# Turning the feed-forward rows with VectorE and a trip through DRAM instead of TensorE

## The chip, the cores and the metric

The kernel runs on one core of a Trainium2 chip. The metric is device time in microseconds (us), from one launch, as the median of repeated runs. The engines are TensorE (PE; its weight loads are listed as PEld), VectorE (DVE), ScalarE (ACT), GpSimd (POOL) and SyncE (SP), which here issues every DMA. Each engine works through its own instructions in the order in which they were written and waits on semaphores.

## The reference, cut to what matters

Eight sequences of 2048 rows of 256 numbers go through one layer: attention with a decay `0.9 ** |n - m|` on the softmax, then a gated feed-forward with 4-bit quantised operands (`F` = 704).

```python
x = x + attention(layernorm(x))
q4 = fp4_quant_dequant            # blocks of 16 along the last dimension
xn = layernorm(x)
h = silu(q4(xn) @ q4(w_gate).T) * (q4(xn) @ q4(w_up).T)      # rows x 704
x = x + q4(h) @ q4(w_down).T                                  # needs q4(h) with its columns on partitions
```

## The kernel before

A first stage (to about 310 us) makes keys, queries and values of all sequences and prepares the weights. Then come 128 tiles of 128 rows (`B` = 8 sequences of `T` = 16 tiles). A product in fp32 precision is made of three passes over an upper and a lower part of each operand (`PASSES`), so every operand that was transposed into PSUM is copied once by ScalarE (`upper`, line 793) and once subtracted by VectorE (`lower`, line 1226).

The tiles are software-pipelined by hand. Every engine has a function `step(at, s)`, called for s = 0 to 15 of each sequence; s - 1 and so on count into the sequence before. What follows is the order of each engine within a step, which is what the argument needs:

- **TensorE**: `attend_begun(s-1)` (transposes of the first two groups of decayed probabilities of tile s-1), `scores(s)` (24 matmuls), then `attend(s-1)`: for each group g of at most four key blocks, wait until its lower part is there (`copied`), its matmuls, and the transposes of group g+2 behind them; `x_transposed(s-2)` comes behind group 0; `h_transposed(s-5, 0)` and `(s-5, 1)` (4 and 2 transposes of the quantised hidden rows `hq`, line 675) come behind later groups. Then `gate_up(s-2)` (18 matmuls, after `xqT` is copied) and `down(s-5)` (17 matmuls, after `hT` is copied).
- **VectorE**: `maxima(s, 0)`, lower parts of groups 0 and 1 of tile s-1, `maxima(s, 1)` with the negated maximum `nmax`, lower part of `xqT`, lower parts of groups 2 and 3, of `hT` (2 instructions), `h_levels(s-3)`, `residual(s-1)`, then `x_scales` and `x_levels(s-1)` with `h_made(s-2)` between them, then `result(s-5)`.
- **ScalarE**: `queries(s+1)`, upper parts of groups 0 and 1, of `xqT`, of the other groups, of `hT` (2 instructions), `exponentials(s)` (two, each from `nmax`), `gate(s-2)` with table loads around it.
- **GpSimd**: `queries(s+1)`, `decays(s)` (after both exponentials of s), `values` in half of the steps, `x_quantised(s-1)` (after `x_levels(s-1)` of VectorE), `h_quantised(s-3)`, which ends with `hq_ready`, `h_scaled(s-2)`.
- **SyncE**: `load_q(s+2)`, value and edge loads, `store(s-5)` after its result, `load_x(s)`.

A sequence of 16 tiles has 8 to 14 key blocks a tile (tile t attends blocks t-7 to t+7; tiles 7 and 8 save one). In groups of four, the tiles 1 to 4 and 11 to 14 have three groups, the tiles 5 to 10 four. Tiles 0 and 15 have 8 blocks in groups of 2, 3 and 3. Three PSUM banks (`RING`) go round for all transposes and the gate and up products.

Of the kernel before, what the change touches and what calls it, by code (L numbers as in the profile page):

```python
# [8 lines left out]
F32 = mybir.dt.float32  # L9
# [37 lines left out]
XR, LAG, LATER = 8, 5, 3  # L47
# [39 lines left out]
def groups(t):  # L87

    bs = blocks_of(t)
    size = CT if 0 < t < T - 1 else CT - 1  # L90
    first = len(bs) % size or size
    return [bs[:first]] + [bs[i:i + size] for i in range(first, len(bs), size)]


def plan_slots():
# [6 lines left out]
    def step(s, has, weights=False):  # L102
# [12 lines left out]
        for g in range(max(len(gs), 1)):  # L115
            if g == 0 and has(s - 2):
                take("xqT", s - 2)
            if g + 2 < len(gs):
                take("pT", s - 1, g + 2)
            for h in range(2):  # L120
                if g == min(max(len(gs) - LATER, 0) + h, max(len(gs), 1) - 1) and has(s - LAG):
                    take("hT", s - LAG, h)
# [16 lines left out]
def build(nc, X, WQ, WK, WV, WG, WU, WD, rot_tab, decay_tab, eye, out):  # L139
# [5 lines left out]
    with ExitStack() as ctx:  # L145
# [17 lines left out]
        q_dram = nc.dram_tensor("q_dram", (B, NC, P, KT, CH), F32, kind="Internal").ap()  # L163

# [7 lines left out]
        hq = [hq_buf[:, i * FT:(i + 1) * FT] for i in range(2)]  # L172
# [50 lines left out]
        probs = sb("probs", [P, L])  # L223

# [31 lines left out]
        hq_step, hv_ready, hg_ready, hq_ready = sem("hq_step"), sem("hv_ready"), sem("hg_ready"), sem("hq_ready")  # L256
        NSTEP_W, NSTEP_LN2, NSTEP_XQ, NSTEP_HQ = 5, 2, 6, 5
# [26 lines left out]
        def tile(at, t):  # L284

            return at[0] * T + t

# [60 lines left out]
        def _(sp):  # L348
# [115 lines left out]

            def step(j, s, is_first, more):
# [37 lines left out]
            for t in range(T - LAG, T):  # L503
                store(B - 1, t)
# [4 lines left out]
        def _(pe):  # L509
# [120 lines left out]
            def attend(at, t, meanwhile, later):  # L630
                if not has(at, t):
                    meanwhile()
                    later(0)
                    later(1)
# [5 lines left out]
                for g, bs in enumerate(gs):  # L640
# [23 lines left out]
                    for h in range(2):  # L664
                        if g == min(max(len(gs) - LATER, 0) + h, len(gs) - 1):
                            later(h)

            def h_transposed(at, t, h):
                if has(at, t):
                    for ks in (range(0, CT), range(CT, HK))[h:h + 1]:  # L670
                        if h == 0:
                            pe.wait_ge(hq_ready, tile(at, t) + 1)
                        dst = slot(at, "hT", t, h)
                        for j, k in enumerate(ks):
                            mm = pe.transpose(dst[:, j * P:(j + 1) * P], hq[t % 2][:, k * P:(k + 1) * P], ident[:])  # L675
                        mm.then_inc(filled, 1)
# [9 lines left out]
            def down(at, t):  # L686
                if has(at, t):
                    copied(at, "hT", t, 1)
# [11 lines left out]
            def step(at, s):  # L700
# [8 lines left out]
                attend(at, s - 1, lambda: x_transposed(at, s - 2), lambda h: h_transposed(at, s - LAG, h))  # L709
# [13 lines left out]
        def _(act):  # L723
# [87 lines left out]
            def h_transposed(at, t):  # L811
                if has(at, t):
                    for h, n in enumerate((CT, HK - CT)):
                        upper(hT[0][:, h * CT:h * CT + n, :].rearrange("p k t -> p (k t)"),
                              bank(at, "hT", t, h)[:, 0:n * P], at, "hT", t, h)
# [43 lines left out]
            def step(at, s):  # L859
# [3 lines left out]
                attend(at, s - 1, range(min(n, 2)))  # L863
                begins = s == 0 and at[2] is first_plan
# [8 lines left out]
                h_transposed(at, s - LAG)  # L873
# [19 lines left out]
        def _(pool):  # L893
# [84 lines left out]
            def decays(at, s, meanwhile):  # L978
# [4 lines left out]
                for g, bs in enumerate(groups(s)):  # L983
# [15 lines left out]
                    op.then_inc(decayed, 1)  # L999

# [14 lines left out]
            def h_quantised(at, t):  # L1015
                if has(at, t):
# [3 lines left out]
                    if has(at, t - 2):  # L1020
                        pool.wait_ge(filled, nth(at, "hT", t - 2, 1) + 1)
# [3 lines left out]
                    pool.tensor_tensor(hq[t % 2][:, F - HALF:FT].rearrange("p (a b k) -> p a b k", a=2, k=QB), last, scale, ALU.mult)  # L1025
# [399 lines left out]
```

## Time and profile before

| | |
|---|---|
| median of 3 runs | 2549.42 us (2548.14 to 2549.66) |
| span of the profiled execution, first to last instruction | 2546.6 us |
| own device time of the profiled execution | not listed; the median is 2.8 us above the span |
| one sequence of 16 tiles in the middle | 275.62 us |
| first stage | about 310 us |
| tail without scores | from 2504 us on |

Groups of rows name line, engine and operation, then output <- input with shapes. Times in a timeline are us from the start of the span. Busy time is the sum of the instructions of an engine; a timeline row that ends in brackets says how long its engine had been idle and what ended that.

### The profile page before, as it was taken

The numbers are of one execution on the slowest core, as the hardware profiler recorded it, in microseconds if no ns is written. First come the engines' busy times: TensorE is split into PE (matmuls) and PEld (weight loads), VectorE is DVE, ScalarE is ACT, GpSimd is POOL, SyncE is SP. The second block draws the span as 40 slices with busy tenths as digits, with TensorE's granted clock in tenths as the row PEclk, the third lists the DMA queues.
The fourth block names the chain that finished last, engine by engine and source line by source line (L and its number), as shares of the span: only waits on it lengthen the run. The fifth ranks groups of instructions, "written<-read, shape, count | busy, mean of one in ns | idle before, by whom it ended". The sixth has DMA issues, their size and how long they took to land.

```text
span 2546.6 us, 51904 instructions
## 1 busy us (share of the span) xinstructions
PE 2518.4 (99%) x16160; PEld 2290.0 (90%) x16160; DVE 2140.9 (84%) x4759; ACT 1489.8 (59%) x2966; POOL 1816.8 (71%) x1929
## 2 busy tenths in 40 slices
PE   8999999999999999999999999999999999999997
PEld 7888879999999999999999999999999999999996
DVE  8999878888878888888888888888888888888886
ACT  5766565656555655566565656565556655555654
POOL 6999956667767676667766776677666776677665
PEclk9999999999999999999999999999999999999999
DMA  8878511122111311131112111131113111211110
GB/s 285 302 271 299 186 50 30 34 86 66 38 40 45 107 37 42 34 106 42 42 34 91 62 38 40 45 107 39 42 34 106 41 42 34 95 58 38 40 38 22
DMA packets 163473, 203.27 MB, mean 80 GB/s; under 512 B 15184, under 2 KB 116752, under 8 KB 163216
## 3 DMA queue, kind: packets, MB, share of 16 engines
q1 hardware_dynamic: 163216, 200.01, 24.1%
q8 instruction: 141, 2.31, 0.4%
q14 instruction: 116, 0.95, 0.1%
HBM read 103.42 MB, written 77.59 MB: 71 GB/s over the span
## 4 chain that ended last, share of the span: by engine, by line
PE 85%; POOL 0%; DVE 0%; issue 0%; ACT 0%; POOLq 0%
PE score L516 27%; PE acc L655 19%; PE ring L516 19%; PE acc L516 9%; PE ring L622 6%; PE ring L675 3%; PE acc L697 1%; PE ring L613 1%; DVE hT L1226 0%; POOL probs L998 0%; ACT probs L823 0%; ACT hT L793 0%; POOL h_buf L1019 0%; POOL xv L1004 0%; POOL h_buf L1013 0%
## 5 line engine op out<-in xcount | busy, mean ns | idle before, releaser
L516 PE MATMUL score<-keys,q_st 128*128 128x512 f32 x3072 | 733.7, 394 | 3.0 <-ACT probs L823 2.6
L516 PEld LDWEIGHTS score<-keys,q_st 128*128 128x128 f32 x3072 | 567.0, 188 | 117.8 <-issue 3.0
L998 POOL TENSOR_TENSOR probs<-probs,decay 128x512 f32<-128x512 f32 (+3 forms) x416 | 450.7, 1097 | 197.5 <-ACT probs L823 197.5
L655 PE MATMUL acc<-vals,pT 128*128 128x256 f32 x3984 | 554.6, 286 | 0.8 <-DVE pT L1226 0.8
L516 PE MATMUL ring<-w_gu,xqT 128*128 128x512 f32 (+1 forms) x2304 | 509.1, 374 | 0.0
L655 PEld LDWEIGHTS acc<-vals,pT 128*128 128x128 f32 x3984 | 498.1, 189 | 7.3 <-DVE pT L1226 2.0
L516 PEld LDWEIGHTS ring<-w_gu,xqT 128*128 128x128 f32 x2304 | 419.0, 188 | 63.6 <-DVE xqT L1226 0.4
L793 ACT ACTIVATE xqT<-ring 128x256 fp32r<-128x256 f32 x128 | 49.3, 385 | 706.9 <-PE ring L613 706.9
L1239 DVE TENSOR_REDUCE smax<-score 128x1 f32<-128x1024 f32 x256 | 312.8, 1222 | 95.6 <-PE score L516 94.1
L1226 DVE TENSOR_TENSOR pT<-ring,pT 128x512 fp32r<-128x512 f32 (+3 forms) x432 | 248.7, 600 | 66.7 <-ACT pT L793 65.5
L1004 POOL TENSOR_TENSOR xv<-xv,xe 128x256 f32<-128x256 f32 x128 | 94.4, 737 | 269.1 <-DVE xv L1079 269.1
L823 ACT ACTIVATE probs<-score,nmax 128x1024 f32<-128x1024 f32 x256 | 282.8, 1116 | 2.1 <-DVE nmax L1242 2.0
L793 ACT ACTIVATE pT<-ring 128x512 fp32r<-128x512 f32 (+3 forms) x432 | 218.7, 527 | 74.8 <-PE ring L622 66.6
L516 PE MATMUL acc<-w_dn,hT 128*128 128x256 f32 x1920 | 240.9, 277 | 4.7 <-DVE hT L1226 4.6
L516 PEld LDWEIGHTS acc<-w_dn,hT 128*128 128x128 f32 x1920 | 236.7, 188 | 5.8 <-DVE hT L1226 5.3
L1019 POOL TENSOR_TENSOR h_buf<-h_buf 128x704 f32<-128x704 f32 x128 | 219.0, 1711 | 4.3 <-DVE h_buf L1079 4.3
L1322 DVE TENSOR_TENSOR h_buf<-h_buf,ring 128x256 f32<-128x256 f32 (+1 forms) x384 | 144.2, 376 | 76.2 <-ACT h_buf L849 76.0
L793 ACT ACTIVATE hT<-ring 128x512 fp32r<-128x512 f32 (+1 forms) x256 | 125.0, 490 | 123.1 <-PE ring L675 123.1
L1226 DVE TENSOR_TENSOR hT<-ring,hT 128x512 fp32r<-128x512 f32 (+1 forms) x256 | 141.3, 553 | 64.9 <-ACT hT L793 64.8
L622 PE MATMUL ring<-ident,probs 128*128 128x128 f32 x1328 | 194.8, 273 | 0.2 <-DVE w_gu L1231 0.2
L516 PE MATMUL score<-xT,w_in 128*128 128x512 f32 x768 | 188.3, 394 | 2.3 <-DVE xT L1107 2.3
L1013 POOL TENSOR_TENSOR h_buf<-h_buf,hrs 128x704 f32<-128x704 f32 x128 | 178.2, 1392 | 0.0
(133 smaller groups left out, 4470.0 us busy)
## 6 DMA issues: line engine op xcount, KB each, us to landing
k_dram<-keys SPq DMA_DIRECT2D x56, 512.0 KB, 4.5
keys<-k_dram SPq DMA_DIRECT2D x56, 512.0 KB, 7.3
edge<-vals SPq DMA_DIRECT2D x288, 64.0 KB, 2.1
q_raw<-q_dram SPq DMA_DIRECT2D x129, 128.0 KB, 2.6
x_in<-X SPq DMA_DIRECT2D x32, 512.0 KB, 4.5
q_dram<-q_stage SPq DMA_DIRECT2D x32, 512.0 KB, 5.4
x_res<-X SPq DMA_DIRECT2D x128, 128.0 KB, 2.1
out<-x_res SPq DMA_DIRECT2D x128, 128.0 KB, 1.7
```

The source lines that it names most:

```text
L516: mm = pe.matmul(dst, stat(a, k), mov(m, k), start=i == 0, stop=ends and i == n - 1)
L622: mm = pe.transpose(dst[:, n * P:(n + 1) * P], source, ident[:])
L655: mm = pe.matmul(pv_out, pT[g % 2][:, a, j * P:(j + 1) * P], edge[places[m]][:] if kb in edges else vals[m][:, kb, :], start=i == 0, stop= ...
L793: act.activation(dst, src, ACT.Copy).then_inc(hi_done, 1)
L823: act.activation(probs[:, h * 2 * CH:(h + 1) * 2 * CH].rearrange("p (j n) -> p j n", j=2), score[:, 2 * h:2 * h + 2, :], ACT.Exp, bias=nma ...
L998: op = pool.tensor_tensor(probs[:, k0:k1], probs[:, k0:k1], decay[:, off + k0:off + k1], ALU.mult)
L1004: pool.tensor_tensor(xv[:], xv[:], xe[:], ALU.subtract).then_inc(x_levelled, 1)
L1013: pool.tensor_tensor(blocks(hv[t % 2]), blocks(hv[t % 2]), spread(hrs[:], HB), ALU.mult).then_inc(hv_ready, 1)
L1019: pool.tensor_tensor(hv[t % 2], hv[t % 2], he[t % 2], ALU.subtract).then_inc(h_levelled, 1)
L1226: dve.tensor_tensor(dst, src, hi.bitcast(F32), ALU.subtract).then_inc(freed, 1)
L1239: dve.tensor_reduce(smax[:, h:h + 1], score[:, 2 * h:2 * h + 2, :], AX.XY, ALU.max).then_inc(maxed, 1)
L1322: dve.tensor_tensor(hv[t % 2][:, p0:p0 + w], silu[t % 2][:, p0:p0 + w], bank(at, "gu", t, p)[:, w:2 * w], ALU.mult).then_inc(freed, 1)
```

## The change

The hidden rows are no longer transposed by TensorE. For each tile: VectorE turns `hq` (128 rows by 768 columns) in blocks of 32 by 32 in one instruction (`h_turned_blocks(s-4)`, between the lower part of group 1 and `maxima(s, 1)`); SyncE writes the result to DRAM, waits for it, and reads it back with four DMAs, one per 32 columns of each chunk, into `hqT` (`rows_turned(s-4)`, behind `load_q(s+2)`); ScalarE makes the upper part of all six chunks in one instruction from SBUF (`h_transposed(s-5)`, now behind groups 0 and 1 and ahead of the exponentials); GpSimd makes the lower part in one instruction (`h_lower(s+1-5)`, behind `decays(s)` and `values` and ahead of `x_quantised(s-1)`). `hq` has one buffer in place of two. Tile 0 has two groups of four.

```diff
-    size = CT if 0 < t < T - 1 else CT - 1
+    size = CT if t < T - 1 else CT - 1
...
+            def rows_turned(j, t):
+                g, i = j * T + t, t % 2
+                sp.wait_ge(h_turned, g + 1)
...
+                sp.dma_start(h_dram[i], h_turn.rearrange("p (c r) -> p c r", c=CT)).then_inc(turn_out, 16)
+                sp.wait_ge(turn_out, (g + 1) * 16)
+                for c in range(CT):
+                    sp.dma_start(hqT[i][c * QUAD:(c + 1) * QUAD, :, :], h_dram[i, :, c, :].rearrange("(a i) r -> i a r", a=CT)).then_inc(hqT_back[i], 16)
...
+                if s >= TURNED or not is_first:
+                    rows_turned(j, s - TURNED)
...
TensorE:
-                            mm = pe.transpose(dst[:, j * P:(j + 1) * P], hq[t % 2][:, k * P:(k + 1) * P], ident[:])
...
-                    copied(at, "hT", t, 1)
+                    pe.wait_ge(h_split, tile(at, t) + 1)
ScalarE, h_transposed(at, t):
-                        upper(hT[0][:, h * CT:h * CT + n, :].rearrange("p k t -> p (k t)"),
-                              bank(at, "hT", t, h)[:, 0:n * P], at, "hT", t, h)
+                    act.wait_ge(hqT_back[t % 2], halves(at, t) * CT * 16)
+                    if has(at, t - 1):
+                        act.wait_ge(dn_done, tile(at, t))
+                    act.activation(chunks(hT[0][:]), quads(hqT[t % 2][:]), ACT.Copy).then_inc(h_upper, 1)
...
                 attend(at, s - 1, range(min(n, 2)))
+                h_transposed(at, s - LAG)
GpSimd:
+            def h_lower(at, t):
+                if has(at, t):
+                    pool.wait_ge(h_upper, tile(at, t) + 1)
+                    pool.tensor_tensor(chunks(hT[1][:]), quads(hqT[t % 2][:]), chunks(hT[0][:]).bitcast(F32), ALU.subtract).then_inc(h_split, 1)
...
+                h_lower(at, s + 1 - LAG)
                 x_quantised(at, s - 1)
                 h_quantised(at, s - 3)
VectorE:
+            def h_turned_blocks(at, t):
+                if has(at, t):
+                    dve.wait_ge(hq_ready, tile(at, t) + 1)
+                    if has(at, t - 1):
+                        dve.wait_ge(turn_out, tile(at, t) * 16)
+                    dve.transpose(h_turn..., hq...).then_inc(h_turned, 1)
...
                 maxima(at, s, 0)
                 attend(at, s - 1, range(min(n, 2)))
+                h_turned_blocks(at, s - TURNED)
                 maxima(at, s, 1)
...
-                for h in range(2):
-                    h_transposed(at, s - LAG, h)
```

## Rows read from the trace of the kernel before

**Rows 1.** The page's busy times and its granted TensorE clock in 40 slices.

```profile
PE 2518.4 (99%) x16160; PEld 2290.0 (90%) x16160; DVE 2140.9 (84%) x4759; ACT 1489.8 (59%) x2966; POOL 1816.8 (71%) x1929
...
PEclk9999999999999999999999999999999999999999
```

**Rows 2.** Windows of one sequence: us, then busy time of each engine.

```profile
1243.50:1519.12 275.62, 275.62 (x1788) 252.24 (x1787) 230.40 (x519) 160.41 (x318) 191.54 (x223) 1.00 0.18 56
```

**Rows 3.** Timeline of the step that attends tile 5: start us, us, engine, line.

```profile
1500.27 0.56 PEld L622 LDWEIGHTS ring<-ident,probs 128*128 128x128 f32 x5
...
1501.26 0.75 ACT L793 ACTIVATE pT<-ring 128x128 fp32r<-128x128 f32 x2
...
1503.90 0.74 POOL L1004 TENSOR_TENSOR xv<-xv,xe 128x256 f32<-128x256 f32 x1 [1.17 <-DVE xv L1079]
...
1505.33 0.63 SPq L382 DMA_DIRECT2D q_raw<-q_dram  x1
...
1506.58 1.22 DVE L1239 TENSOR_REDUCE smax<-score 128x1 f32<-128x1024 f32 x1 [0.51 <-PE score L516]
...
1507.58 1.28 POOL L1026 TENSOR_TENSOR hq_buf<-h_buf,hs 128x640 f32<-128x640 f32 x1
...
1508.31 0.68 DVE L1226 TENSOR_TENSOR pT<-ring,pT 128x512 fp32r<-128x512 f32 x1
...
1509.11 0.47 PEld L675 LDWEIGHTS ring<-ident,hq_buf 128*128 128x128 f32 x4
...
1509.54 1.48 PEld L655 LDWEIGHTS acc<-vals,pT 128*128 128x128 f32 x12
...
1510.97 0.24 PEld L675 LDWEIGHTS ring<-ident,hq_buf 128*128 128x128 f32 x2
...
1512.44 3.75 PEld L516 LDWEIGHTS ring<-w_gu,xqT 128*128 128x128 f32 x18
...
1518.21 0.67 PEld L622 LDWEIGHTS ring<-ident,probs 128*128 128x128 f32 x6
```

**Rows 4.** Groups by line and shape: busy us, mean ns; then idle time before them.

```profile
L941 POOL TENSOR_TENSOR q_st<-q_raw,q_st 128x256 fp32r<-128x256 f32 x129 | 95.5, 741 | 0.7 <-ACT q_st L780 0.7
...
L968 POOL TENSOR_TENSOR vals<-v_raw,vals 128x512 fp32r<-128x512 f32 x59 | 79.6, 1349 | 0.0
...
L857 ACT ACTIVATE vals<-v_raw 128x512 fp32r<-128x512 f32 x59 | 36.4, 618 | 0.0
L748 ACT ACTIVATE keys<-rot_k 128x1024 fp32r<-128x1024 f32 x32 | 33.5, 1047 | 12.6 <-POOL rot_k L906 12.6
...
L1072 DVE TENSOR_SCALAR h_buf<-h_buf 128x704 int32<-128x704 int32 x128 | 72.1, 563 | 5.7 <-POOL h_buf L1013 5.5
...
L1079 DVE SCALAR_TENSOR_TENSOR h_buf<-h_buf 128x704 f32<-128x704 f32 x128 | 115.3, 900 | 4.4
```

**Rows 5.** Longest waits of that sequence: us in total, times, longest us.

```profile
POOL xv L1004 <- DVE xv L1079: 33.3, 16, 2.9
```

**Rows 6.** DMA issues of the page: KB each, median us to landing.

```profile
q_dram<-q_stage SPq DMA_DIRECT2D x32, 512.0 KB, 5.4
...
out<-x_res SPq DMA_DIRECT2D x128, 128.0 KB, 1.7
...
v_dram<-v_stage SPq DMA_DIRECT2D x28, 512.0 KB, 2.9
```

**Rows 7.** Tail: two timeline rows behind idle stretches of TensorE.

```profile
2507.14 0.50 PE L655 MATMUL acc<-edge,pT 128*128 128x256 f32 x2 [2.17 <-DVE pT L1226]
...
2522.02 0.44 PE L613 MATMUL ring<-ident,xq 128*128 128x128 f32 x2 [4.27 <-POOL xq L1008]
...
2523.45 4.95 PEld L516 LDWEIGHTS ring<-w_gu,xqT 128*128 128x128 f32 x18 [0.39 <-DVE xqT L1226]
```

**Rows 8.** Windows of TensorE there: us, busy, granted clock.

```profile
2523.00:2524.00 1.00, 0.98 (x4) 0.50 0.00 0
...
2526.00:2527.00 1.00, 1.00 (x5) 0.99 0.00 0
```

More of the change, by code:

```diff
@@ L46 @@
 RING = 3
[L47 removed]
+XR, LAG, TURNED = 8, 5, 4
+QUAD = 32
 W_SLOTS = 3
@@ L170, in build @@
         silu = he
-        hq = [hq_buf[:, i * FT:(i + 1) * FT] for i in range(2)]
+        hq, h_turn = (hq_buf[:, i * FT:(i + 1) * FT] for i in range(2))
         xv, xe, xq = sb("xv", [P, D]), sb("xe", [P, D]), sb("xq", [P, D])
@@ L223, in build @@
         probs = sb("probs", [P, L])
+        hqT = [sb(f"hqT{i}", [P, CT, HK * QUAD]) for i in range(2)]
         score = ctx.enter_context(nc.psum_tensor("score", [P, 4, CH], F32))
@@ L256, in build @@
         hq_step, hv_ready, hg_ready, hq_ready = sem("hq_step"), sem("hv_ready"), sem("hg_ready"), sem("hq_ready")
+        sp_passed, h_turned, turn_out, hqT_back, h_upper, h_split = sem("sp_passed"), sem("h_turned"), sem("turn_out"), [sem(f"hqT_back{i}") for i in range(2)], sem("h_upper"), sem("h_split")
         NSTEP_W, NSTEP_LN2, NSTEP_XQ, NSTEP_HQ = 5, 2, 6, 5
@@ L286, in tile, with halves, quads, chunks @@
             return at[0] * T + t
+        def halves(at, t):
+            return at[0] * (T // 2) + t // 2 + 1
+        def quads(ap):
+            return ap.rearrange("p a (k j) -> p k a j", j=QUAD)
+        def chunks(ap):
+            return ap.rearrange("p k (a j) -> p k a j", j=QUAD)
         def nth(at, *key):
@@ L502, in _ @@
                 step(B - 1, s, False, False)
-            for t in range(T - LAG, T):
-                store(B - 1, t)
+            for s in range(T, T + LAG):
+                if s - TURNED < T:
+                    rows_turned(B - 1, s - TURNED)
+                store(B - 1, s - LAG)
             for i in range(XR):
@@ L663, in attend @@
                         group(at, t, g + 2)
[L664 to L674, printed above, removed]
-                            mm = pe.transpose(dst[:, j * P:(j + 1) * P], hq[t % 2][:, k * P:(k + 1) * P], ident[:])
-                        mm.then_inc(filled, 1)
             def gate_up(at, t):
@@ L999, in decays @@
                     op.then_inc(decayed, 1)
+                if len(groups(s)) <= 2:
+                    meanwhile()
             def x_quantised(at, t):
@@ L1252, in attend @@
                     lower(pT[g % 2][:, 1, 0:n], bank(at, "pT", t, g)[:, 0:n], pT[g % 2][:, 0, 0:n], at, "pT", t, g)
-            def h_transposed(at, t, h):
+            def h_turned_blocks(at, t):
                 if has(at, t):
-                    for n in (CT, HK - CT)[h:h + 1]:
-                        hi, lo = (hT[i][:, h * CT:h * CT + n, :].rearrange("p k t -> p (k t)") for i in range(2))
-                        lower(lo, bank(at, "hT", t, h)[:, 0:n * P], hi, at, "hT", t, h)
+                    dve.wait_ge(hq_ready, tile(at, t) + 1)
+                    if has(at, t - 1):
+                        dve.wait_ge(turn_out, tile(at, t) * 16)
+                    dve.transpose(h_turn.rearrange("p (c k j) -> p k c j", c=CT, j=QUAD), hq.rearrange("p (k c i) -> p k c i", c=CT, i=QUAD)).then_inc(h_turned, 1)
             def residual(at, t):
```

25 lines of the change are left out of this document (12 added, 13 removed).

## The prediction, as put on record

> **What bounds the kernel now.** I read the page's busy times first: TensorE is busy 99% of the span at full granted clock, VectorE 84%, GpSimd 71% [rows 1]. The windows then show one sequence in the middle with TensorE busy for all of its 275.62 us, against 230.40 on VectorE and 191.54 on GpSimd [rows 2]. So TensorE's work alone sets the pace, and whatever leaves it is a gain if nobody else becomes late. Whether that holds is decided by the order in the queues, so I read the timeline of one step next [rows 3]. It runs from 1500.27 (first transposes of the step) to 1518.21 (those of the next), 17.94 us. Below, +x is x us after 1500.27.
>
> **What is removed.** The six transposes take TensorE 0.43 us (1509.11 to 1509.54) and 0.21 us (1510.97 to 1511.18, where the next matmuls begin), together 0.65 us [rows 3]. Over 128 tiles that is at most 83 us. Two ScalarE and two VectorE instructions go too; neither engine bounds.
> The Trainium skill (VectorE: DVE Perf Modes, The three transpose paths) gives 390 ns for one 128 by 128 transpose on TensorE. Six would be 2.34 us a tile and the relief 300 us; the row, where the next instruction follows after 0.11 us each, decides, and the sum does not use the page.
>
> **Where the new instructions stand.** The turn stands in VectorE's queue ahead of `maxima(s, 1)`. It needs `hq_ready` of tile s-4, which GpSimd gives at the end of `h_quantised` in its own step s-1. In the timeline that is the work that begins with `x_quantised` at 1503.90 and ends with line 1026 at 1508.86: +8.6 [rows 3]. `maxima(s, 1)` starts today at 1506.58, +6.3. Hence even with nothing else moved VectorE waits 2.3 us with the turn at its head. The old transposes used the `hq` one tile older, so TensorE never felt this. Queued behind the turn are the maximum, `nmax` (and with it both exponentials), the lower part of `xqT`, and those of groups 2 and 3. TensorE stops at group 2, which has no slack: its lower part was ready at 1508.99 and group 2 began at 1509.54 behind transposes that are now gone [rows 3].
>
> The second new wait is on GpSimd. `h_lower` stands ahead of `x_quantised` and needs ScalarE's upper part, which ScalarE reaches only after the upper parts of groups 0 and 1 of the same step. Today GpSimd sits idle before `x_quantised` for 33.3 us in 16 steps, 2.1 each [rows 5], so on busy time alone `h_lower` looks free. It comes too late to use that idle time: it starts when the idle time is nearly over.
>
> **The loop.** These orders close a circle through one step, and the step cannot be shorter. From the first transposes of a step:
> - ScalarE has done groups 0 and 1 at +1.74 in this step [rows 3]; where groups differ I take +1.6 on the whole.
> - The upper part of `hT`, 768 columns from SBUF: between 618 ns (512) and 1047 (1024) [rows 4], 0.83, with the handover 0.88: +2.5.
> - `h_lower`, 768 columns, two full inputs: 741 ns for 256 and 1349 for 512 [rows 4] give 2.4 ns a column; the straight line gives 1.95, a little less at the larger size: 1.9, with handover 1.95: +4.4. `x_levels` ends at +3.6 today and no longer decides.
> - `x_quantised` and `h_quantised` unchanged, 1503.90 to 1508.86: 4.96, with handover 5.0: +9.4.
> - The turn. No row shows one. Bounds by VectorE's 704-column rows: 563 ns (two columns at a time) and 900 ns (one at a time) [rows 4], scaled to 768: 0.61 and 0.98. I take 0.95, since every column passes the array once: +10.4. The Trainium skill (Vector Engine (DVE) Microarchitecture Reference, The reshape front-end and per-opcode configuration) says that the 32 by 32 transpose sustains one element per cycle per lane, which would exclude the lower bound; no run here shows it yet.
> - From the start of `maxima(s, 1)` (1506.58) to the end of the lower part of group 2 (1508.99): 2.41 [rows 3]: +12.85 with the handover. TensorE has finished its scores, groups 0 and 1 and the transposes by about +9, and idles some 4 us.
> - The rest of TensorE's step: groups 2 and 3, 1509.54 to 1512.44 less the 0.21 of two old transposes, 2.7; gate, up and down, 1512.44 to 1518.21, 5.77 [rows 3].
>
> So a step with four groups takes 12.85 + 2.7 + 5.77 = 21.3 us. With three groups (11 matmuls at 0.12, by 1.48 for 12 [rows 3]) it is 12.85 + 1.35 + 5.77 = 19.95. Tile 15 (9 matmuls) gives 19.7. Tile 0 has no group 2, and its gate waits for `xqT`, 0.68 earlier: 18.0 rounded. A sequence is 6 x 21.3 + 8 x 19.95 + 19.7 + 18.0 = 325.1 us against 275.6 [rows 2]: 49.5 more, 3.09 a step. The turn begins in step 4, so 124 steps with scores pay: 384 us. The 0.65 us are inside this; they come out of TensorE's share ahead of the stall and only lengthen its wait.
>
> **The trip through DRAM.** After the turn at +10.4: issue and write of 384 KB. Bounds 1.7 us (128 KB) and 5.4 (512 KB in the busy first stage), and 2.9 for 512 KB nearest [rows 6]; I take 3.5 with the issue. Four issues at about 0.63 [rows 3] and landing in 1.7 to 2.9 [rows 6]: back at about +19. ScalarE wants it at +1.6 of the next step, 21.5 to 22.9. It is hidden with 2.5 to 4 us to spare; without that cover each us is paid 1:1. SyncE holds its later loads about 8 us longer; edges and rows are wanted only in the next step. In the tail one such trip lies open: +8.
>
> **The clock.** In the tail TensorE idled 4.27 us [rows 7] and then had a granted clock of 0.50, the 1.2 GHz level, until 2526.0 [rows 8]. The 18 weight loads of gate and up took 4.95 us there in place of 3.75, and with the transposes ahead it cost 1.4. Behind 2.17 us of idling nothing fell. The new stall is between 3.1 us (tile 0) and 4.5 (tile 15), so it will fall in some steps. I take one in four: 31 x 1.4 = 43 us; ends 0 and all 124, 174.
>
> **Sum.** The profiled span 2546.6 + 384 + 8 + 43 = 2982, and 2.8 us lie around the span: 2985 us, 17% slower. Bounds of the unknown costs, per step: turn -0.35 or +0.03, upper part -0.2 or +0.2, lower part -0.4 (if it went at the line from 256 columns without growth in cost) or +0.5 (strided input), together -0.95 to +0.7: -118 to +87 us; the clock -43 to +131.
>
> **Rivals.**
> - *The loop with the clock falling in nearly every step*: 2985 + 131, about 3115. For it: idle stretches near 4.27. Against: most are shorter. 0.12.
> - *The lower part is not in the circle* (ScalarE reaches the upper part early enough that GpSimd's idle time takes `h_lower` in). With `hq_ready` at today's +8.6, group 2 is ready at +12.05 in place of +12.85, and each us by which `x_levels` comes earlier, once TensorE stalls behind it, is one more, up to the 2.1 of idling: 124 x (0.8 to 2.9) is 100 to 360 us less, 2625 to 2885, say 2760. Against it: the order of ScalarE's queue. 0.07.
> - *The trip through DRAM bounds*: write 5.4 and reading 7 us would bring the data back at +24.8; the point from which it decides is +21.5 for short steps, and the price is 124 x 3 to 5: 3200 to 3500. Against it: DMA engines are at a share of 0.18 in the sequence [rows 2]. 0.08.
> - *Faster: TensorE's 0.65 us come back whole.* If `hq_ready` came before `maxima(s, 1)`, that is 2.3 us earlier than today and with `h_lower` done in GpSimd's 2.1 us of idling, TensorE would still be the bound: 2549 - 83 = 2466, or some 2490 with group 2 waiting for its lower part by 0.2 us. For it: busy time, where GpSimd has 5 us a step free. It decides only if `hq_ready` is at +6.3 or sooner. 0.05.
>
> **Chances.** My forecast, the loop with the clock falling sometimes, 0.64, its own range 2870 to 3075; the rivals 0.12, 0.07, 0.08 and 0.05; something else 0.04. A difference under 0.2% cannot be told from none in this kernel. Faster 0.05, within 0.2% 0.02, slower 0.93. The range that leaves out 2 in 10 is 2860 to 3130; it takes in the bounds of the turn and of the two `hT` parts and the clock, and leaves out the DRAM-bound, most of the short-loop case and the fast case.
>
> **What would show it.** In the changed profile: TensorE's share falls to about 85%, its largest idle group is line 655 waiting for the lower part `pT` (about 4 us in each step) and for tile 0 the gate's; VectorE waits for GpSimd's `hq` ahead of the turn, and GpSimd's `h_lower` waits for ScalarE's upper part; the chain that ended last goes round through GpSimd, VectorE and TensorE; a sequence takes about 325 us; the turn is near 0.95 us, `h_lower` near 1.9. I am wrong if the turn's wait for `hq` is near zero, if `h_lower` starts before +2, or if ScalarE waits for the DMA.

## The result, and the profile after

The changed kernel takes 3181.74 us (median of 4 runs, 3174.35 to 3186.09) against 2549.54 for the kernel before (4 runs). The ratio is 1.2475, 95% interval 1.2455 to 1.2494: a quarter slower. The forecast of 2985 has the direction; the time is 197 us above it and lies outside the range (2860 to 3130).

These are lines of the changed kernel's page: busy times, granted TensorE clock in 40 slices, the chain that ended last by engine, three groups (busy and mean ns, then idle time before them and its releaser) and the DMA issues (KB each, us to landing).

```profile
PE 2712.7 (85%) x15392; PEld 2433.8 (76%) x15392; DVE 2080.8 (65%) x4623; ACT 1519.8 (48%) x2830; POOL 2084.8 (66%) x2049
...
PEclk9999999989889888898888989889898888889897
...
POOL 34%; issue 24%; PE 16%; DVE 12%; ACT 2%; DMA 1%; POOLq 1%; DVEq 0%; SPq 0%; ACTq 0%
...
L687 PE MATMUL acc<-vals,pT 128*128 128x256 f32 x3984 | 692.8, 335 | 394.6 <-DVE pT L1254 392.1
...
L1053 POOL TENSOR_TENSOR hT<-hqT,hT 128x768 fp32r<-128x768 f32 x128 | 238.5, 1863 | 489.8 <-ACT hT L835 489.8
...
L1287 DVE STREAM_TRANSPOSE hq_buf<-hq_buf 128x768 f32<-128x768 f32 x128 | 125.2, 978 | 457.9 <-POOL hq_buf L1048 457.9
...
h_dram<-hq_buf SPq DMA_DIRECT2D x128, 384.0 KB, 2.3
hqT<-h_dram SPq DMA_DIRECT2D x512, 96.0 KB, 2.2
```

Against [rows 1], TensorE's share went from 99% to 85%, and no other engine took its place: VectorE stands at 65% and GpSimd at 66%. No engine is full, so a chain of waits sets the pace, and the third line shows it going round through GpSimd, TensorE and VectorE. The waits are in the group rows: the turn (line 1287) behind GpSimd's `hq`, `h_lower` (line 1053) behind ScalarE's upper part, TensorE (line 687) behind the lower part `pT`. Digits of 8 in the clock line stand where [rows 1] have only 9; the mean clock of the profiled run is 0.903, against 0.999 before.

The waits of the same kernel, us in total, times, longest:

```profile
POOL hT L1053 <- ACT hT L835: 489.8, 128, 9.6
DVE hq_buf L1287 <- POOL hq_buf L1048: 457.9, 128, 9.5
PE acc L687 <- DVE pT L1254: 393.3, 121, 4.8
```

The stalls come in 121 to 128 of 128 tiles, so this is not a matter of some bad steps. One step in the timeline, that which attends tile 1 (three groups). It begins at 1732.52, so +x is x us after that:

```profile
1732.52 0.56 PEld L656 LDWEIGHTS ring<-ident,probs 128*128 128x128 f32 x5
...
1733.86 0.83 ACT L835 ACTIVATE hT<-hqT 128x768 fp32r<-128x768 f32 x1
...
1734.77 1.87 POOL L1053 TENSOR_TENSOR hT<-hqT,hT 128x768 fp32r<-128x768 f32 x1 [2.43 <-ACT hT L835]
...
1740.24 1.28 POOL L1048 TENSOR_TENSOR hq_buf<-h_buf,hs 128x640 f32<-128x640 f32 x1
...
1741.65 0.98 DVE L1287 STREAM_TRANSPOSE hq_buf<-hq_buf 128x768 f32<-128x768 f32 x1 [3.52 <-POOL hq_buf L1048]
...
1744.24 0.68 DVE L1254 TENSOR_TENSOR pT<-ring,pT 128x512 fp32r<-128x512 f32 x1
...
1745.05 1.51 PE L687 MATMUL acc<-vals,pT 128*128 128x256 f32 x9 [3.82 <-DVE pT L1254]
...
1746.58 5.09 PEld L550 LDWEIGHTS ring<-w_gu,xqT 128*128 128x128 f32 x18
```

Reading the ends off as start plus duration: upper part of `hT` +2.2, `h_lower` +4.1, `hq_ready` +9.0, turn +10.1, group 2 on TensorE +12.5. The prediction had +2.5, +4.4, +9.4, +10.4 and +12.85. The circle is the one it described, and each part of it has about the size it gave. The last row is the surprise: the same 18 weight loads took 3.75 us in [rows 3]. The windows of that stretch (us; busy time of PE, PEld, DVE, ACT, POOL; granted clock; DMA share; GB/s) say why:

```profile
1745.00:1746.00 1.00, 0.95 (x8) 0.96 (x9) 0.93 (x3) 1.00 (x3) 0.00 (x0) 1.00 0.00 0
1746.00:1747.00 1.00, 1.00 (x7) 1.00 (x6) 0.91 (x2) 0.95 (x4) 0.60 (x1) 0.51 0.56 162
1747.00:1748.00 1.00, 1.00 (x3) 0.78 (x3) 0.87 (x2) 0.95 (x1) 1.00 (x2) 0.50 0.77 205
1748.00:1749.00 1.00, 1.00 (x4) 0.73 (x3) 0.37 (x4) 0.00 (x0) 1.00 (x2) 0.50 0.53 148
1749.00:1750.00 1.00, 1.00 (x5) 0.82 (x4) 0.00 (x0) 0.41 (x2) 0.92 (x4) 0.79 0.04 9
```

Behind 3.82 us of idling the clock was at 0.50, the 1.2 GHz level, from 1746 until within 1749, with TensorE busy all the time. That is what the tail showed after 4.27 us [rows 7, 8]; here it happens in the loop.

It happens nearly everywhere. Between 395 and 3105 us, that is in nearly all the steps with a turn, TensorE has 123 idle stretches of over 2 us, about one a step. The clock fell behind 113 of them, and the shortest of these was 2.71 us. It stayed at 0.50 for some 3.4 us in 60 steps and for some 6.8 in 53. Behind the other ten, of 2.77 to 2.87 us, it did not fall. Seven of the ten are the step that attends tile 11; here its group 2, and the window of TensorE alone that follows (busy, granted clock, DMA share, GB/s):

```profile
1972.33 1.65 PE L687 MATMUL acc<-vals,pT 128*128 128x256 f32 x12 [2.87 <-DVE pT L1254]
...
1972.33:1980.33 8.00, 8.00 (x55) 1.00 0.35 98
```

So the length of a stall alone does not tell whether the clock falls: 2.71 us did it, 2.87 us did not.

Worked out from TensorE's timeline, from the first score weights of one step to those of the next, for the sequence around it, in us; "filled" is the third experiment below, and the last line says how long the clock was at half speed in each step of the changed kernel (the share missing in the granted clock of the step's window, twice):

```
attended tile  15    0    1    2    3    4    5    6    7    8    9   10   11   12   13   14    sum
before       15.7 15.7 16.2 16.7 17.2 17.2 18.1 18.4 18.5 18.5 18.3 18.3 17.4 16.9 16.5 16.1  275.6
forecast     19.7 18.0 19.95 (four times)  21.3 (six times)              19.95 (four times)     325.1
filled       22.7 17.7 20.7 19.7 19.9 19.6 21.0 21.0 21.1 21.2 21.0 21.7 19.9 19.7 19.6 19.6  326.1
after        23.9 19.3 21.3 21.3 22.7 21.2 22.5 22.5 23.9 23.9 23.8 24.2 19.9 21.1 22.3 21.2  354.9
half clock    6.7  3.5  3.4  3.4  6.8  3.4  3.6  3.6  6.7  6.7  6.7  6.8  0.0  3.4  6.7  3.4   74.8
```

The filled kernel follows the forecast. The one step after without a fall of the clock, tile 11, is as long as the filled one and as the forecast. A fall of some 3.4 us costs 1.4 to 1.6 us in most steps, one of some 6.7 us 2.5 to 2.8. The exceptions are tile 15, where part of the slow time falls into the idle stretch, and tile 1 (0.6).

### The profile page after: what moved, and what is told of

It is laid out like the page before. It is cut to its first block, busy times and chain, and to the rows that moved or that the text cites. A ratio compares the mean times of both kernels' runs of the same rounds, so it can differ in the third digit from the quotient of the medians.

```text
span 3181.6 us, 50694 instructions
## 1 busy us (share of the span) xinstructions
PE 2712.7 (85%) x15392; PEld 2433.8 (76%) x15392; DVE 2080.8 (65%) x4623; ACT 1519.8 (48%) x2830; POOL 2084.8 (66%) x2049
## 4 chain that ended last, share of the span: by engine, by line
POOL 34%; issue 24%; PE 16%; DVE 12%; ACT 2%; DMA 1%; POOLq 1%; DVEq 0%; SPq 0%; ACTq 0%
PE acc L687 9%; POOL h_buf L1041 7%; POOL hT L1053 6%; POOL probs L1018 6%; POOL hq_buf L1048 5%; DVE smax L1267 5%; PE ring L550 4%; POOL xv L1026 3%; POOL xq L1030 2%; DVE pT L1254 2%; POOL rstd L994 2%; POOL vals L988 2%; PE acc L550 2%; DVE x_res L1300 1%; DVE st L1302 1%
## 5 line engine op out<-in xcount | busy, mean ns | idle before, releaser
L687 PE MATMUL acc<-vals,pT 128*128 128x256 f32 x3984 | 692.8, 335 | 394.6 <-DVE pT L1254 392.1
L687 PEld LDWEIGHTS acc<-vals,pT 128*128 128x128 f32 x3984 | 631.1, 237 | 426.7 <-DVE pT L1254 366.8
L1018 POOL TENSOR_TENSOR probs<-probs,decay 128x512 f32<-128x512 f32 (+3 forms) x408 | 477.6, 1183 | 215.2 <-ACT probs L843 215.2
L550 PE MATMUL ring<-w_gu,xqT 128*128 128x512 f32 (+1 forms) x2304 | 591.7, 416 | 23.1 <-DVE xqT L1254 23.1
L550 PEld LDWEIGHTS ring<-w_gu,xqT 128*128 128x128 f32 x2304 | 488.4, 220 | 109.8 <-DVE xqT L1254 24.9
L1053 POOL TENSOR_TENSOR hT<-hqT,hT 128x768 fp32r<-128x768 f32 x128 | 238.5, 1863 | 489.8 <-ACT hT L835 489.8
L1287 DVE STREAM_TRANSPOSE hq_buf<-hq_buf 128x768 f32<-128x768 f32 x128 | 125.2, 978 | 457.9 <-POOL hq_buf L1048 457.9
L869 ACT ACTIVATE h_buf<-ring 128x256 f32<-128x256 f32 (+1 forms) x384 | 140.8, 367 | 379.7 <-PE ring L550 378.2
L1254 DVE TENSOR_TENSOR pT<-ring,pT 128x512 fp32r<-128x512 f32 (+3 forms) x424 | 242.0, 605 | 0.2 <-ACT pT L812 0.2
```

The source lines that it names most:

```text
L550: mm = pe.matmul(dst, stat(a, k), mov(m, k), start=i == 0, stop=ends and i == n - 1)
L687: mm = pe.matmul(pv_out, pT[g % 2][:, a, j * P:(j + 1) * P], edge[places[m]][:] if kb in edges else vals[m][:, kb, :], start=i == 0, stop= ...
L869: act.activation(silu[t % 2][:, p0:p0 + w], bank(at, "gu", t, p)[:, 0:w], ACT.Silu).then_inc(hi_done, 1)
L1018: op = pool.tensor_tensor(probs[:, k0:k1], probs[:, k0:k1], decay[:, off + k0:off + k1], ALU.mult)
L1053: pool.tensor_tensor(chunks(hT[1][:]), quads(hqT[t % 2][:]), chunks(hT[0][:]).bitcast(F32), ALU.subtract).then_inc(h_split, 1)
L1254: dve.tensor_tensor(dst, src, hi.bitcast(F32), ALU.subtract).then_inc(freed, 1)
```

## The experiments

Line numbers are those of the changed kernel; some shift by a few in an experiment. "Before" was run beside each on the same chip, with medians of 2549.4 to 2551.0. Parts that are only moved or left out are shown as the calls in `step`.

**The turn alone in the kernel before.** The six TensorE transposes stay, nothing goes through DRAM, and the turn writes a spare buffer. GpSimd also waits, before it writes `hq` again, until the turn has read it.

```diff
 VectorE:
                 attend(at, s - 1, range(min(n, 2)))
+                h_turned_blocks(at, s - 4)
                 maxima(at, s, 1)
```

> The kernel before with one instruction added: VectorE turns hq of tile s-4 into a spare buffer ahead of maxima(s, 1), and nobody reads it; the six transposes of TensorE stay. My theory (the wait of the turn for hq_ready at the head of VectorE's queue is a cause on its own, without h_lower and without DMAs): slower, 2650 to 2850, with group 2 of TensorE waiting for its lower part. Rival (only the moved lower part or the transfers cost): 2549 to 2560, since VectorE has 1 us a step free.

Measured: 2811.68 us, ratio 1.1027 (1.1005 to 1.1049). This is what was expected (2650 to 2850). VectorE waited for GpSimd's `hq` at the turn for 263.0 us in 127 waits. A useless instruction of 979 ns, which over 128 tiles is 125 us of an engine with 16% of the span free [rows 1], costs 262 us at this place. TensorE waits for the copies queued behind it, for that of `xqT` alone 143.5 us in 106 waits.

**The turn moved behind the lower parts.** In the changed kernel.

```diff
 VectorE:
-                h_turned_blocks(at, s - TURNED)
                 maxima(at, s, 1)
...
+                h_turned_blocks(at, s - TURNED)
                 h_levels(at, s - 3)
```

> The changed kernel with one instruction moved: VectorE's turn of hq stands behind the lower parts of the groups 2 and 3 instead of ahead of maxima(s, 1). My theory (the turn, waiting at the head of VectorE's queue for hq_ready, holds up nmax and the lower part of group 2): the loop through VectorE is gone, TensorE does not stall, its clock stays up, and the 0.65 us of transposes a step come back less about 0.2 us of waiting for group 2: 2549 - 83 + 26 = 2492, range 2470 to 2560. Rival A (GpSimd's h_lower ahead of x_quantised holds up the step by itself): over 2650. Rival B (the trip through DRAM bounds): over 2700, since the turn comes no earlier.

Measured: 2723.44 us, ratio 1.0664 (1.0644 to 1.0684), mean clock 0.976. This takes back 458 of 632 us, but not to the level of before: TensorE's `down` now waited for VectorE's `residual` (62.4 us in 48 waits), and `h_lower` still waited for ScalarE (225.7 us). The theory that the turn's place is all of it (2470 to 2560) fell. The time fits rival A, and by its number rival B too; the run without the trip, further on, decides between them.

**The stall filled with matmuls.** TensorE repeats up to 24 matmuls of `vals` in front of group 2 in each step of the changed kernel; nothing else is touched.

```diff
 TensorE, attend:
+                def again(g, bs, times):
+                    for r in range(times):
+                        for j, kb in enumerate(bs):
+                            for a, m in PASSES if kb not in edges else ():
+                                pe.matmul(pv_out, vals[0][:, kb, 0:P], vals[0][:, kb, :], start=False, stop=False)
```

> The changed kernel, and in each step TensorE gets up to 24 more matmuls of 256 columns behind the transposes of group 3 (behind group 0 in tile 0), 2.9 us of work that lies in the stall; they add products of the values with themselves to the attention output, so its numbers change. Theory of the clock (the part of the loss that my sum missed is TensorE at 1.2 GHz behind nearly every stall): the granted clock stays at 1.00, and although there is more work the time falls by 124 x 1.5 to 2 us, to 2930 to 3000. Rival (the missing part lies elsewhere, in the instructions or the transfers): 3180 or more.

Measured: 2974.3 us, ratio 1.1658 (1.1634 to 1.1681). With 2976 more matmuls the kernel is 207 us faster, inside the 2930 to 3000 expected. Its page (busy times, clock) and TensorE's weight loads in one step:

```profile
PE 2840.6 (96%) x18368; PEld 2581.2 (87%) x18368; DVE 2122.5 (71%) x4623; ACT 1517.3 (51%) x2830; POOL 2089.2 (70%) x2049
...
PEclk9999999999999999999999999999999999999997
```

```profile
1704.82 2.94 PEld L677 LDWEIGHTS acc<-vals 128*128 128x128 f32 x24
1707.88 1.12 PEld L696 LDWEIGHTS acc<-vals,pT 128*128 128x128 f32 x9
1708.93 0.31 PEld L696 LDWEIGHTS acc<-edge,pT 128*128 128x128 f32 x2
1709.16 3.76 PEld L550 LDWEIGHTS ring<-w_gu,xqT 128*128 128x128 f32 x18
```

The added loads (line 677) lie inside the wait, the clock stays up, and gate and up take 3.76 us again. So the clock costs at least some 207 us of the 632; I call it a lower bound, because a part of the added work may itself delay group 2. An estimate from above: a mean clock of 0.903 over 3181.6 us is 617 us at half speed, and a TensorE that was busy in all of it would have lost half, 309 us. In the table above this kernel's steps are the forecast's within 0.4 us, but for tiles 15 and 1.

**`h_lower` moved behind `h_scaled`.** In the changed kernel, with the turn left in its place.

```diff
 GpSimd:
-                h_lower(at, s + 1 - LAG)
                 x_quantised(at, s - 1)
                 h_quantised(at, s - 3)
                 h_scaled(at, s - 2)
+                h_lower(at, s + 1 - LAG)
```

> The changed kernel with h_lower moved on GpSimd from ahead of x_quantised to behind h_scaled; the turn stays where it is. My theory: hq_ready comes 2 to 3 us earlier in a step, still later than the end of the scores, so the stall shrinks from 3.5 us to 0.5 to 2 us and the clock falls in few steps: 2600 to 2800, say 2680. Rival A (h_lower alone is the cause): down to 2550 or less. Rival C (the place of h_lower does not matter): 3180 stays.

Measured: 2712.42 us, ratio 1.0631 (1.0608 to 1.0654). It lies in the expected 2600 to 2800. The turn's wait for `hq` fell from 457.9 to 178.9 us and TensorE's for `pT` from 393.3 to 152.8. Most of the loss thus needs both of the two waits: taking either away gives back 458 or 469 us, together more than the 632 there are. They are in one circle, not in a sum.

**Both moved.** The two edits together.

```diff
-                h_turned_blocks(at, s - TURNED)      # VectorE, ahead of maxima(s, 1)
+                h_turned_blocks(at, s - TURNED)      # VectorE, ahead of h_levels(s - 3)
-                h_lower(at, s + 1 - LAG)             # GpSimd, ahead of x_quantised(s - 1)
+                h_lower(at, s + 1 - LAG)             # GpSimd, behind h_scaled(s - 2)
```

> Both moves together: the turn behind the lower parts of groups 2 and 3, h_lower behind h_scaled. My theory: TensorE bounds, 2480 to 2500, equal to the run with the turn alone moved within 15 us, faster than the kernel before. Rival A (h_lower matters by itself): this run is faster than the one with the turn alone moved by over 50 us. Rival B (the trip through DRAM bounds): over 2549.

Measured: 2607.27 us, ratio 1.0216 (1.0199 to 1.0233). The circle is open (the turn now waits for `hq` 8.3 us in 11 waits), and the kernel is still 2% slower than before, where 2480 to 2500 was expected. TensorE waits for the residual ahead of `down` for 36.9 us in 44 waits, a wait that is not in the list of the kernel before. Its timeline:

```profile
1502.53 1.87 POOL L1053 TENSOR_TENSOR hT<-hqT,hT 128x768 fp32r<-128x768 f32 x1
1502.96 1.82 DVE L1100 TENSOR_SCALAR h_buf<-h_buf 128x704 int32<-128x704 int32 x1
...
1504.81 0.95 DVE L1103 TENSOR_SCALAR h_buf<-h_buf 128x704 f32<-128x704 f32 x1
...
1505.34 3.45 POOL L1018 TENSOR_TENSOR probs<-probs,decay 128x512 f32<-128x512 f32 x2
...
1505.79 1.86 DVE L1107 SCALAR_TENSOR_TENSOR h_buf<-h_buf 128x704 f32<-128x704 f32 x1
...
1507.76 0.48 DVE L1300 SCALAR_TENSOR_TENSOR x_res<-acc,rinv,x_res 128x256 f32<-128x256 f32 x1
...
1508.39 2.00 PE L550 MATMUL acc<-w_dn,hT 128*128 128x256 f32 x15 [0.77 <-DVE x_res L1300]
```

Line 1100 takes 1.82 us while GpSimd's `h_lower` runs beside it, and line 1107 1.86 us beside the decays, for 563 and 900 ns in [rows 4]. The residual on which `down` waits is queued behind them. In the groups by line and shape of this kernel:

```profile
L1100 DVE TENSOR_SCALAR h_buf<-h_buf 128x704 int32<-128x704 int32 x128 | 172.0, 1344 | 5.2 <-POOL h_buf L1035 5.1
...
L1107 DVE SCALAR_TENSOR_TENSOR h_buf<-h_buf 128x704 f32<-128x704 f32 x128 | 157.4, 1229 | 4.4
```

**Next, 32 of the 768 columns in the lower part.** The order of the last kernel; GpSimd's work is cut, and TensorE reads the upper part in its place (as many matmuls, other numbers).

```diff
-pool.tensor_tensor(chunks(hT[1][:]), quads(hqT[t % 2][:]), chunks(hT[0][:]).bitcast(F32), ALU.subtract)
+pool.tensor_tensor(hT[1][:, 0, 0:QUAD], hqT[t % 2][:, 0, 0:QUAD], hT[0][:, 0, 0:QUAD].bitcast(F32), ALU.subtract)
```

> The run with both instructions late (2607 us), and GpSimd makes only 32 of the 768 columns of the lower part; TensorE uses the upper part in its place (same matmuls, other numbers). There the three instructions of h_levels on VectorE took 1344, 907 and 1229 ns beside a busy GpSimd, against 563, 549 and 900 before. Theory of the shared access (GpSimd's 1.9 us of h_lower fall on h_levels, slow them by 1.5 us a step, and the residual and the down product behind them come late): the three return to about 560, 550 and 900, and the time falls to 2470 to 2500, TensorE bound. Rival (VectorE's order or the DMA trip keeps TensorE waiting): 2560 to 2607, and the three stay slow.

Measured: 2562.05 us, ratio 1.0045 (1.0029 to 1.0062), 45 us less than with all columns, and still not faster than before; 2470 to 2500 was expected. From the first scores to the last it takes as long as the kernel before (2177.3 us against 2176.4), though its borders take 20.4 to 22.5 us for 15.7; what is left is the tail, 71.6 us against 58.0. Line 1100 went back to 534 ns: the same instruction in the same place, slowed only by what GpSimd did beside it. Line 1107 stayed at 1228, with the decays still beside it:

```profile
L1107 DVE SCALAR_TENSOR_TENSOR h_buf<-h_buf 128x704 f32<-128x704 f32 x128 | 157.2, 1228 | 4.4
...
L1100 DVE TENSOR_SCALAR h_buf<-h_buf 128x704 int32<-128x704 int32 x128 | 68.4, 534 | 2.7 <-POOL h_buf L1035 2.6
```

**The lower part on VectorE.** As both moved, but VectorE makes the lower part ahead of `maxima(s, 1)`.

```diff
 GpSimd:
-                h_lower(at, s + 1 - LAG)
 VectorE:
+                h_lower(at, s - LAG)
                 maxima(at, s, 1)
```

> The run with both late, with the lower part made by VectorE (one instruction of 768 columns ahead of maxima(s, 1), where it waits for TensorE anyway) and not by GpSimd; output as the reference's. Theory of the shared access: GpSimd is idle again during h_levels, these return to about 560, 550 and 900 ns, VectorE pays 1 us for the lower part, part of it in its idle time: 2490 to 2560. Rival (VectorE becomes the bound): 2600 or more.

Measured: 2622.17 us, ratio 1.0285 (1.0268 to 1.0302). That is the rival's time (2600 or more; 2490 to 2560 was expected). The instruction of line 1100 takes 577 ns again, with GpSimd's subtraction gone from beside it, but the lower part takes VectorE 1414 ns, where 1 us was reckoned with. VectorE is 90% busy and TensorE waits for its `pT` again (53.4 us in 65 waits). The lower part has no free place there either.

**The residual ahead of `h_levels`.** As both moved, with the last four key loads of a sequence split so that two of them stand behind the write to `h_dram`; first the split alone, then with the residual moved too.

```diff
 VectorE:
                 h_turned_blocks(at, s - TURNED)
+                residual(at, s - 1)
                 h_levels(at, s - 3)
-                residual(at, s - 1)
```

> The run with both late (2607 us) with one change of order on SyncE: of the last 2 MB of keys of a sequence, 1 MB is loaded ahead of the trip as before and 1 MB only behind the write of the turned rows. Nothing is left out. Theory (the write of the trip stands behind 2 MB of keys, which makes the border step 2 to 4 us longer): 2580 to 2600. Rival (the border is long for another reason, or the keys then come too late for the scores): 2605 or more.

> As the run with the keys split, and on VectorE residual(s-1) goes ahead of h_levels(s-3). Nothing is left out. In the run with both late TensorE waited 0.7 us for the residual ahead of the down product in 44 steps, since h_levels in front of it is slowed by GpSimd's lower part; with the residual ahead that wait goes, and h_levels runs beside other work. Theory of the shared access: 20 to 50 us below the run with the keys split, so 2540 to 2575, about the kernel before. Rival (h_levels then delays x_levels by as much): no gain, 2580 to 2600.

Measured: 2606.75 us with the split alone, ratio 1.0226 (1.0211 to 1.0242): it does nothing. With the residual 2569.38 us, ratio 1.0077 (1.0063 to 1.0090): 37 us less, as expected, and as much as TensorE had waited for the residual. That shows by another way that the slowed instructions of VectorE cost through the residual queued behind them. Sequences now take some 276 us against 275.6: steps with four groups take 17.7 to 18.3 us in place of 18.1 to 18.5, and that is given back at the border between sequences, 18.7 to 20.0 for 15.7 (the first one 16.9), and with tile 3, 18.3 for 17.2. Of the 20 us that are left, the tail has 16: 74.4 us from the last scores to the end against 58.0. TensorE there:

```profile
2541.05 0.39 PE L718 MATMUL acc<-w_dn,hT 128*128 128x256 f32 x2
2546.48 3.57 PE L552 MATMUL acc<-w_dn,hT 128*128 128x256 f32 x15 [5.04 <-POOL hT L1055]
...
2553.66 3.57 PE L552 MATMUL acc<-w_dn,hT 128*128 128x256 f32 x15 [3.19 <-POOL hT L1055]
...
2561.68 3.57 PE L552 MATMUL acc<-w_dn,hT 128*128 128x256 f32 x15 [4.03 <-POOL hT L1055]
```

The last three tiles, 7.2 and 8.0 us apart, each waiting 3.2 to 5.0 us for `hT` at half clock (the 15 matmuls take 3.57 us, 1.96 before); in the kernel before these waits are 1.52 us each.

**Edges ahead of the keys.** As both moved, with the residual first, the keys in one piece, and in the last step of a sequence the edge loads issued ahead of the keys.

```diff
 SyncE:
                 if last and more:
+                    load_edges(j, s, is_first)
                     load_keys(j, 1)
...
-                load_edges(j, s, is_first)
+                if not (last and more):
+                    load_edges(j, s, is_first)
```

> The run with residual first (2569 us) with the keys in their old order again (2 MB ahead of the trip) and, in the last step of each sequence, the two edge loads of SyncE ahead of those keys instead of behind the trip. Nothing is left out. In the profile of that run the border step took 18.7 to 20 us: TensorE waited 2.4 us for the edges and 1.1 us for the last keys. Theory (the border is long because small loads that TensorE needs stand behind 4 MB of keys and the trip): seven borders, 2 to 3.5 us each, 2545 to 2557, the time of the kernel before. Rival (only the place of the keys matters): 2570 or more.

Measured: 2569.66 us, ratio 1.0081 (1.0067 to 1.0095): no gain. 2545 to 2557 was expected. The border step stays at 19.2 to 19.6 us (the first one 16.8). TensorE's waits for the edges are gone from the list (its weight loads had 10.5 us in 5 waits), but ScalarE's for `hqT` went up from 36.9 to 60.3 us, 10 waits each: the edges came earlier and the trip later. Whether that exchange is what holds the border no run shows.

**The changed kernel without the trip.** The five DMAs are left out, ScalarE and GpSimd read `h_turn` itself, and the turn waits until GpSimd has read the tile before.

```diff
 SyncE:
-                    rows_turned(j, s - TURNED)
 ScalarE and GpSimd: quads(hqT[t % 2][:])  ->  quads(h_turn...)
```

> The changed kernel without the trip through DRAM: the five DMAs of a tile are left out, ScalarE and GpSimd read VectorE's turned block straight away (so the blocks stay in their partitions and the output is not the reference's). Everything else keeps its place. My theory: the trip is hidden in the steps but for one in each sequence, where the write of 384 KB stands behind the loads of the next keys and ScalarE waited 2.5 us: 15 to 60 us less than 3182, so 3120 to 3165. Rival (the trip or its queueing on SyncE is a large part of the loss): below 3100.

Measured: 3116.48 us, ratio 1.2234 (1.2212 to 1.2255), 65 us less than the change: just below the expected 3120 to 3165 and above the rival's 3100, so the trip is not what bounds the kernel. The border step falls from 23.2 to 24.0 us to 20.9, 7 times, and the tail from 93.0 to 84.5; that is about 28 us. The other 37 are in steps inside the sequences, some shorter by 1.2 to 2.9 us and a few longer (tile 11 by up to 2.6, where the clock now falls). The mean clock is 0.918 in place of 0.903. Worked out from these, the time at half clock goes from 617 to 511 us, 106 less, which is worth up to 53 us; that covers the 37, but no run separates it. What happens at the border is in the changed kernel's timeline:

```profile
1675.55 3.25 SPq L446 DMA_DIRECT2D keys<-k_dram  x4
1679.01 0.44 SPq L490 DMA_DIRECT2D h_dram<-hq_buf  x1
1687.67 2.98 SPq L493 DMA_DIRECT2D hqT<-h_dram  x4
...
1693.15 0.85 ACT L835 ACTIVATE hT<-hqT 128x768 fp32r<-128x768 f32 x1 [2.48 <-DMA hqT<-h_dram]
1694.08 1.87 POOL L1053 TENSOR_TENSOR hT<-hqT,hT 128x768 fp32r<-128x768 f32 x1 [7.63 <-ACT hT L835]
```

The write of 384 KB stands behind key loads of 512 KB each. It is 8.66 us from its issue to the first read, for a landing of 2.3 us at the median, and ScalarE waits for the data.

**The little lower part without the trip.** The two edits together: 32 columns, and both readers at `h_turn`; the turn waits for the lower part of the tile before.

```diff
 VectorE, h_turned_blocks:
-                        dve.wait_ge(turn_out, tile(at, t) * 16)
+                        dve.wait_ge(h_split, tile(at, t))
```

> The run with both instructions late and only 32 columns of the lower part (2562 us), now also without the trip through DRAM (blocks stay in their partitions; other numbers). There, one step in each sequence took 20.4 to 22.5 us, in the kernel before 15.7, with edges and hqT waiting for DMAs. Theory (the trip and the loads of the next keys hold each other up at the border of two sequences, 5 to 6 us each): seven borders, 35 to 45 us less, 2515 to 2527. Rival (something else at the border): 2555 to 2565. Neither reaches 2466, as group 2 waits for its lower part in the wider tiles.

Measured: 2569.64 us, ratio 1.0078 (1.0063 to 1.0093), 8 us more than with the trip. 2515 to 2527 was expected. The border step fell from 20.4 to 22.5 us to 17.3 to 17.5 (the first one 19.5), but the step behind it grew from 14.7 to 16.7, and with `hqT` gone the turn must wait until GpSimd has read the last tile (50.6 us in 44 waits). The experiment put a new wait in the place of the old and says nothing on the sum.

## Why the prediction was wrong in its size

**What held.** That TensorE's time sets the pace only as long as nobody is late; that the turn waits for `hq_ready` at the head of VectorE's queue (457.9 us); that `h_lower` closes a circle through ScalarE and GpSimd (489.8 us), and that moving either opens it. The loop: forecast 325.1 us for a sequence, 326.1 with the clock held up, of which some 3 belong to the border. The prices: turn 978 ns for 0.95, upper part 840 for 0.83, lower part 1863 for 1.9. The turn's 978 ns for 768 columns lie at the upper bound of the sum; the rule of the Trainium skill (Vector Engine (DVE) Microarchitecture Reference, The reshape front-end and per-opcode configuration) of one element per cycle and lane excluded the lower one, and this agrees. The 390 ns that the prediction quotes from the Trainium skill (VectorE: DVE Perf Modes, The three transpose paths) is the page's figure for bf16, while the transposes here are fp32; it entered no sum.

**The step that failed is the clock term**: "I take one in four: 31 x 1.4 = 43 us". Filling the stall took off 207 us. It was too small twice, in the number of falls and in the price of one.

The number: the fall was taken to be rare because most stalls are shorter than the 4.27 us of [rows 7]. It came in 113 of 123 steps, behind 2.71 us and more. Between 2.17 (no fall, [rows 7]) and 4.27 no row of before decided, so one in four was a guess. Nor is 2.17 a limit: with both moved, the clock fell behind 1.91 us of idling (at 613.19). The price: 1.4 us came from the one fall in the tail, and it is right for the falls of some 3.4 us. Nearly half of the falls in the loop last twice as long. Behind 3.16 us of idling that began at 1784.5 the clock was at 0.50 from 1787 to past 1793, and that step is 2.8 us over the filled kernel's.

So even the rival "in nearly every step", 3115, was low, though its mechanism is the one that came. The rival on the trip, 3200 to 3500, lies nearer by its number, but the trip is worth 65 us. The prediction's own bounds, the cost terms at their highest and a fall in every step, add up to 2985 + 87 + 131 = 3203 and held the measured time; the range was cut at 3130. Two figures in it have no working: the -0.4 us for the lower part, which no row gives, and the "+24.8" of the rival on the trip, whose terms, 10.4 + 5.4 + 7, make 22.8 without the issues. Neither changes the account.

**Two smaller terms.** The trip through DRAM was called hidden, with 2.5 to 4 us to spare, and the rival against it was marked down on the DMA engines' mean share of 0.18 [rows 2]. One of the prediction's own signs of being wrong did come: ScalarE waited for the data of the trip, 39.2 us in 9 waits, the longest 12.9. A mean over a sequence does not show its border, where the keys of the next one are loaded ahead of the write. In the tail the trip costs 8.5 us (93.0 less 84.5 without it), as forecast (8). The second term, the rest of the new order in the tail, was put at nothing without a reason: turn, upper and lower part of one tile run one after the other, with nothing beside them. Even without the trip TensorE waits 2.87, 4.92 and 2.92 us ahead of the last three `down`, for 1.52 each before, and its 15 matmuls then take about 3.5 us at half clock. With the trip the last two waits are 9.97 and 9.77 us.

Set against the forecast for the span (2982, measured 3181.6), with the filled kernel (span 2971.6) between the two:

| | forecast | measured |
|---|---|---|
| clock: after less filled | 43 | 210 |
| loop, 123 steps between scores, borders taken at 19.7 us | 380 | 370 |
| 7 borders, 22.2 to 24.6 us in the filled kernel | 0 | 23 |
| tail behind the last scores, filled less before (89.7 less 58.0) | 11 (trip 8, one step 3.09) | 32 |
| sum | 434 | 635 |

The sum of the measured column is what the span grew by. Its rows go by where the time shows up, not by cause: the trip's 65 us lie partly in the borders and the tail and partly in the clock's row.

**The other side.** The rival "faster" gave 2466 to 2490 if `hq_ready` came in time. With the turn and `h_lower` both out of the way it still took 2607 us, because GpSimd's lower part and VectorE's `h_levels` slow each other and the residual is queued behind them: 45 us come off with the small lower part, 37 with the residual moved, so this cause is shown from two sides. The small lower part also spares GpSimd 1.6 us a step, and the two runs do not say how much of the 45 that is. The 20 us that the best version then stays above before are the tail's (16) and a few of the sequences. In steps with four groups only 0.2 to 0.4 of TensorE's 0.65 us came back, and the border takes 3 to 4 us a sequence. That the rest of the 0.65 is lost because group 2 waits for its lower part I only argue, and what holds the border step, neither the split of the keys nor the order of the edges showed. No version beat the kernel before; the best of those that leave nothing out is 612 us faster than the change and 0.8% slower than before.

Left open as well: what the trip costs with the clock held up, since the changed kernel with the stall filled and without the trip was not tried, and where between 207 us and the estimate of 309 the clock's cost really is.

## What to carry to other kernels

An engine's free share says nothing about an instruction's place: ask when its input is ready, and who is queued behind it; the same turn waited 457.9 us for its input at one place and 8.3 us at another (with `h_lower` late too). Price a stall on TensorE twice, once for its length and once for the slower clock behind it, and where the trace has no stall of that length, carry both ends of that price into the range and do not cut them off. Look for a new transfer's cover at the borders of the loop and in the tail, where large loads are queued ahead and nothing runs beside it, and price an instruction that moves to GpSimd together with what VectorE runs at that moment.

## What the runs showed of the hardware

- In the changed kernel's loop the clock fell to the 1.2 GHz level behind 113 of 123 idle stretches, from 2.71 us up, and stayed there for some 3.4 or 6.8 us. It did not fall behind ten of 2.77 to 2.87 us. With both moved it fell behind 1.91 us. Useless matmuls in the stall made the kernel 207 us faster.
- A VectorE instruction on 704 columns took 1.82 us beside GpSimd's 768-column subtraction (1344 ns on average), and 534 ns on average with that cut to 32 columns (577 with the subtraction on VectorE). The decays of GpSimd, two instructions of 512 columns, took 3.45 us beside VectorE's line 1107; one of them averaged 1.30 in the kernel before.
- A write of 384 KB queued behind key loads from the same engine could be read back only 8.66 us after its issue; the median landing was 2.3.
